# First attention of a two-layer vision tower: the last three iterations written out by hand, with other PSUM banks for the last groups' norm products

## The reference, cut to what matters

```python
tokens = jnp.einsum('bpi,hi->bph', patches, W) + b
...
logits = jnp.einsum('bhid,bhjd->bhij', q, k) * scale
logits = jnp.einsum('bhij,gh->bgij', logits, w_pre)
attn = jax.nn.softmax(logits, axis=-1)
attn = jnp.einsum('bhij,gh->bgij', attn, w_post)
out = jnp.einsum('bhij,bhjd->bhid', attn, v)
out = out.transpose(0, 2, 1, 3).reshape(b, n, dim)
return out @ w_out.T + b_out
...
m = jnp.mean(x, axis=axis, keepdims=True)
v = jnp.var(x, axis=axis, keepdims=True)
return (x - m) / jnp.sqrt(v + eps)
```

## Time and profile before

| | us |
|---|---|
| median of 3 runs | 844.15 (841.25 to 845.89) |
| the profiled execution | 846.13 |
| its span | 844.3 |
| mean granted PE clock over the span | 0.811 of full speed |

### The profile page before, as it was taken

How to read it: one execution, slowest core, us unless ns; L and a number is a source line. 1 busy time by engine, 2 the same in 40 slices (tenths; PEclk the granted TensorE clock), 3 DMA queues, 4 the chain that set the end, 5 groups by cost and what they waited for, 6 DMA issues and landing times. The chain is left out here.

```text
span 844.3 us, 21253 instructions
## 1 busy us (share of the span) xinstructions
PE 646.9 (77%) x8455; PEld 528.0 (63%) x8455; DVE 504.6 (60%) x904; ACT 349.2 (41%) x871; POOL 224.6 (27%) x254
## 2 busy tenths in 40 slices
PE   2999999999999996750799767778688888982002
PEld 2888888888888875540774556567577777761001
DVE  0375666666666665436214888768577777755862
ACT  0113444444444444230353333432566666765600
POOL 1263333333333333000000233210443333330001
PEclk9999999999999998555559987655688888875555
DMA  8443332333333100016940800000000000001200
GB/s 350 171 174 116 116 117 114 114 114 125 120 132 125 69 2 2 1 47 154 151 60 0 103 0 0 1 0 0 2 3 2 0 0 0 2 2 50 71 8 4
DMA packets 28659, 55.36 MB, mean 66 GB/s; under 512 B 12274, under 2 KB 25698, under 8 KB 26114
## 3 DMA queue, kind: packets, MB, share of 16 engines
q1 hardware_dynamic: 28515, 54.62, 21.8%
q0 software_dynamic: 96, 0.07, 0.0%
HBM read 48.14 MB, written 6.55 MB: 65 GB/s over the span
## 5 line engine op out<-in xcount | busy, mean ns | idle before, releaser
L375 PE MATMUL a_bank<-a_x,a_tok_w 128*128 128x256 f32 (+1 forms) x608 | 151.0, 391 | 15.7 <-DVE a_ht L555 15.7
L375 PEld LDWEIGHTS a_bank<-a_x,a_tok_w 128*128 128x128 f32 (+1 forms) x608 | 113.4, 192 | 37.4 <-DMA tables<-in_tables 15.7
L124 POOL TENSOR_TENSOR a_qt<-a_qp,data 128x512 f32<-128x512 f32 x64 | 71.8, 1153 | 2.1 <-POOL a_qp L617 1.6
L617 POOL TENSOR_TENSOR a_qp<-a_rope 128x260 f32<-128x260 f32 x16 | 11.7, 733 | 176.0 <-DVE a_rope L499 176.0
L1360 ACT ACTIVATE b_at<-b_bank 65x512 f32<-65x512 f32 x64 | 34.9, 602 | 42.7 <-PE b_bank L1207 42.7
L282 ACT ACTIVATE a_at<-a_bank 65x256 f32<-65x256 f32 x128 | 38.9, 390 | 26.8 <-PE a_bank L259 26.8
L493 DVE SCALAR_TENSOR_TENSOR a_ht<-a_bank,data 128x256 f32<-128x256 f32 x16 | 7.7, 484 | 64.9 <-PE a_bank L375 64.9
L259 PE MATMUL a_bank<-a_mix,a_e 64*65 64x64 f32 x1024 | 41.5, 237 | 0.0
L1444 POOL TENSOR_TENSOR b_e<-b_e,b_inv 128x585 f32<-128x585 f32 (+1 forms) x32 | 35.5, 1108 | 20.1 <-DVE b_inv L1295 19.9
L259 PEld LDWEIGHTS a_bank<-a_mix,a_e 64*65 64x65 f32 x1024 | 36.8, 149 | 4.0 <-issue 3.4
L1268 DVE TENSOR_TENSOR b_e<-b_scores,tables 128x520 f32<-128x520 f32 x32 | 20.9, 696 | 29.2 <-PE b_scores L1169 29.2
(11 more groups left out here) (251 smaller groups left out, 1552.8 us busy)
## 6 DMA issues: line engine op xcount, KB each, us to landing
a_x<-in_x SPq DMA_DIRECT2D x16, 2304.0 KB, 7.9
lag_rows<-r_kernel SPq DMA_DIRECT2D x1, 4192.5 KB, 39.0
lags<-lag_rows SPq DMA_DIRECT2D x1, 2112.5 KB
base<-places SPq DMA_DIRECT2D x1, 2080.0 KB
out<-e_plain SPq DMA_DIRECT2D x16, 130.0 KB
expert_weights<-in_w SPq DMA_DIRECT2D x2, 1024.0 KB, 5.9
a_tok_w<-in_tok_w SPq DMA_DIRECT2D x1, 1152.0 KB, 6.6
data<-in_data SPq DMA_DIRECT2D x1, 910.5 KB, 4.6
```

Source lines behind the costliest of these rows:

```text
L124: nc.gpsimd.tensor_tensor(qt[:, b * BLOCKS * P:(b + 1) * BLOCKS * P].rearrange("p (c h i) -> p c h i", i=qb, h=HEADS), wide(by_image[:, b, ...
L375: mm = nc.tensor.matmul(banks[0][:, 0:GP], w[0:rows, k * DIM:(k + 1) * DIM], x[p][0:rows, k * GP:(k + 1) * GP], start=(k == 0), stop=(k == ...
```

## The change

The pipeline generator now ends after iteration 13 on PE, DVE and ACT (POOL and SP keep theirs). What iterations 14, 15 and 16 held is written out by hand, with n = 15. No step is added or dropped; the order of steps on each engine is another, and the banks are:

- output projection, mean and variance of group 13 and of group 15 in bank 0, those of group 14 in bank 2; values of group 15 in bank 6; the last-row mix of 14 and 15 in bank 7, columns 384 on (`late_bank`);
- `centre` of group 15 writes into `rope[0]` (`late_zc`) instead of `zc`;
- helpers take the bank as an argument, `spread` is split into `square` and `root`.

The diff, cut to the part that is written out:

```diff
+            def output(g, bank):
+                pe.wait_ge(S.ot_ready, g + 1)
+                product(bank, D("wo"), ot[:, :]).then_inc(S.y_done, 1)
+
+            def mix_last_rows(g, bank):
+                pe.wait_ge(S.probs_ready, g + 1)
+                nc.tensor.matmul(bank, e[g % 2][:, SLOTS - 1, :], mix_last[:, :], start=True, stop=True).then_inc(S.mixed, 1)
...
                     values_of_image(nc, 3, at, vs[p], banks[7]).then_inc(S.av_done, 1)
 
+            n = GROUPS - 1
+            pe.wait_ge(S.qt_ready, 5 * (n + 1))
+            pe.wait_ge(S.kt_ready, n + 1)
+            pe.wait_ge(S.log_saved, n - 2)
+            scores_of_group(nc, n, seq, qt, kt, S)
+            pe.wait_ge(S.ht_ready, n + 1)
+            output(n - 2, 0)
+
+            pe.wait_ge(S.z_ready, n - 2)
+            pe.wait_ge(S.centred, n - 2)
+            pe.wait_ge(S.sd_ready, n - 2)
+            pe.wait_ge(S.v_ready, n)
+            mix_last_rows(n - 1, late_bank)
+            mix_pair(nc, pe, n - 1, 0, e[0], mix, banks[4:6], S)
+
+            pe.wait_ge(S.tok_saved, n - 2)
+            values(n, ht[1], tokens_bank)
+            pe.wait_ge(S.at_ready, 9 * (n - 1) + 5)
+            mix_pair(nc, pe, n - 1, 1, e[0], mix, banks[4:6], S)
+            values_of_image(nc, 0, at, vs[0], banks[7])
+            values_of_image(nc, 1, at, vs[0], banks[7])
+            mean(n - 2, 0)
+            pe.wait_ge(S.at_ready, 9 * (n - 1) + 9)
+            values_of_image(nc, 2, at, vs[0], banks[7])
+            values_of_image(nc, 3, at, vs[0], banks[7]).then_inc(S.av_done, 1)
+            var(n - 2, 0)
+
+            pe.wait_ge(S.shifted, 3 * n + 3)
+            output(n - 1, 2)
+            mix_last_rows(n, late_bank)
+            mix_pair(nc, pe, n, 0, e[1], mix, banks[4:6], S)
+            mean(n - 1, 2)
+            pe.wait_ge(S.at_ready, 9 * n + 5)
+            mix_pair(nc, pe, n, 1, e[1], mix, banks[4:6], S)
+            pe.wait_ge(S.v_ready, n + 1)
+            values_of_image(nc, 0, at, vs[1], banks[7])
+            values_of_image(nc, 1, at, vs[1], banks[7])
+            tail(n - 2)
+            pe.wait_ge(S.at_ready, 9 * n + 9)
+            values_of_image(nc, 2, at, vs[1], banks[7])
+            values_of_image(nc, 3, at, vs[1], banks[7]).then_inc(S.av_done, 1)
+            var(n - 1, 2)
+
+            pe.wait_ge(S.sd_ready, n - 1)
+            output(n, 0)
+            mean(n, 0)
+            pe.wait_ge(S.tok_saved, n - 1)
+            tail(n - 1)
+            var(n, 0)
+            pe.wait_ge(S.tok_saved, n)
+            tail(n)
+
...
+            n = GROUPS - 1
+            shift_scores(nc, dve, n, seq, e[1], mx, S, 3)
+            residual(n - 2, 0)
+            values(n, 1, tokens_bank)
+            normalise(nc, dve, n, e[1], total, inv, S)
+            centre(n - 2, 0)
+            residual(n - 1, 2)
+            scale(n - 2)
+            save_logits(n - 2)
+            centre(n - 1, 2)
+            residual(n, 0)
+
+            dve.wait_ge(S.q_sum, GROUPS)
+            centre(n, 0, late_zc)
+            scale(n - 1)
+            save_logits(n - 1)
+            scale(n, late_zc)
+            save_logits(n)
+
...
+            n = GROUPS - 1
+            late_zc = rope[0][:, :, :].rearrange("p b t -> p (b t)")
+            save_last(n - 1, late_bank)
+            save_pair(nc, act, n - 1, 0, banks[4:6], at, S)
+            exp_of_group(nc, act, n, e[1], S)
+            save_pair(nc, act, n - 1, 1, banks[4:6], at, S)
+            save_heads(nc, act, n - 1, banks[7], ot, S)
+            square(n - 2)
+            root(n - 2, 0)
+            save_last(n, late_bank)
+            save_pair(nc, act, n, 0, banks[4:6], at, S)
+            save_pair(nc, act, n, 1, banks[4:6], at, S)
+            square(n - 1)
+            save_heads(nc, act, n, banks[7], ot, S)
+            root(n - 1, 2)
+            save_tokens(n - 2)
+            square(n, late_zc)
+            act.wait_ge(S.inverse, n)
+            root(n, 0)
+            save_tokens(n - 1)
+            save_tokens(n)
```

More of the change, by code:

```diff
@@ L339, in embed_and_attend @@
         logit_bank = banks[1][0:TOKENS, 448:448 + GI * EXPERTS0]
+        late_bank = banks[7][0:TOKENS, 384:384 + GI * HEADS]
         x_sem = [S.x0, S.x1]
@@ L422, in _ @@
             pe.wait_ge(S.wmade, 33)
-            for g, i, p in pipeline(pe, 3, GROUPS + 1):
+            for g, i, p in pipeline(pe, 3, GROUPS - 2):
                 flat = ht[p][:, :, :].rearrange("p b t -> p (b t)")
@@ L515, in rotate_keys, with values @@
                                         rope[3][:, :, :], ALU.add).then_inc(S.kt_ready, 1)
-            def values(g, p):
+            def values(g, p, bank=values_bank):
                 dve.wait_ge(S.v_done, g + 1)
@@ L559, in _ @@
             dve.wait_ge(S.v_cleared, 2)
-            for g, i, p in pipeline(dve, 3, GROUPS + 1):
+            for g, i, p in pipeline(dve, 3, GROUPS - 2):
                 if exists(g + 1):
@@ L578, in _, with square, root, save_last @@
                     tokens(g + 3, 1 - p)
+            n = GROUPS - 1
[15 more added lines that the diff above has]
+            save_logits(n)
         @block.scalar
         def _(act):
-            def spread(g):
+            def square(g, zc=zc):
                 act.wait_ge(S.centred, g + 1)
                 nc.scalar.activation(sq[:, :], zc[:, :], ACT.Square).then_inc(S.squared, 1)
+            def root(g, bank=5):
                 act.wait_ge(S.var_done, g + 1)
-                nc.scalar.activation(sd[:, :], banks[5][:, 0:GT], ACT.Sqrt, bias=R.eps[:, :]).then_inc(S.sd_ready, 1)
+                nc.scalar.activation(sd[:, :], banks[bank][:, 0:GT], ACT.Sqrt, bias=R.eps[:, :]).then_inc(S.sd_ready, 1)
+            def save_last(g, bank):
+                act.wait_ge(S.mixed, 3 * g + 1)
+                wait_past(act, S.av_done, g)
+                nc.scalar.activation(at[0:TOKENS, :, :, PATCHES], bank.rearrange("t (b h) -> t b h", b=GI),
+                                     ACT.Copy).then_inc(S.at_ready, 1)
             def save_tokens(g):
@@ L593, in _ @@
             act.wait_ge(S.v_cleared, 3)
-            for g, i, p in pipeline(act, 1, GROUPS + 1):
+            for g, i, p in pipeline(act, 1, GROUPS - 2):
                 if exists(g + 1):
@@ L597, in _ @@
                 if exists(g - 1):
-                    spread(g - 1)
+                    square(g - 1)
+                    root(g - 1)
                 if exists(g):
-                    act.wait_ge(S.mixed, 3 * g + 1)
-                    wait_past(act, S.av_done, g)
-                    nc.scalar.activation(at[0:TOKENS, :, :, PATCHES], lastbank.rearrange("t (b h) -> t b h", b=GI),
-                                         ACT.Copy).then_inc(S.at_ready, 1)
+                    save_last(g, lastbank)
                     save_pair(nc, act, g, 0, banks[4:6], at, S)
```

25 lines of the change are left out of this document (13 added, 12 removed).

## The result

The changed kernel takes 835.29 us (median of 4 runs, 834.32 to 836.74), the kernel before 844.75 beside it (841.25 to 845.89). The ratio is 0.9893, with a 95% interval of 0.9870 to 0.9916: some 9 us faster. A second measurement of the same kernel gave 834.47 against 844.99, ratio 0.9874 (0.9857 to 0.9890). The forecast was 839.5, with a range of 834.5 to 843.3. The direction and the range hold; the gain is twice the forecast. All ratios here leave out slow executions; there was one, of the experiment exp_fill, at 1059.66 us with a granted clock of 0.55 (its median is 829.68 with it, 829.53 without it).

What follows compares the result with a forecast made beforehand. No engine was the bound; PE, DVE and ACT waited on each other, with PE's clock second. The walk fell from 375.06 to 370.36, 4.7 us gained; 846.13 less 4.7 and 1.98 to the median gave 839.5, range 834.5 to 843.3.

Steps and rivals of the forecast that it cites:

- What bounds the stage: Iterations 14 to 16, 331.26 to 375.74: no engine is the bound; PE, DVE and ACT hand work to each other.
- Costs of the steps at a given clock: Each engine's new list walked with traced durations and 0.04 us per hop; the old order's walk ends at 375.06.
- walk for PE at 1.00 to the end: If PE stays at 2.4 GHz to the stage's end, the walk ends at 362.9, gain 12.1 us.
- First leg: Group 15's scores at 331.26 to its probabilities at 342.6, PE at 2.4 GHz: 0.5 us later than before.
- The table switch: ACT's table load before exp of 15: taken as 1.28 us, at most 1.62; rival of dearer switch, chance 0.04.
- The drain: The skill page adds about 1.38 us per table switch; not used in the forecast, with it 840.9.
- Second and third leg: Second: to the logits of 13, copied by 353.8, PE the path. Third: norms of 14 and 15, to 370.36.
- I take the clock as falling here, at 344.5: Behind the projection of 14 PE's clock falls, later pieces cost 1.2 GHz prices; gain 4.7 us.
- a clock of 1.00 through 345 to 352: Named sign, in the new trace, that the forecast is wrong.
- the rival that I had given 0.25 and 836.0: PE's packed work keeps its clock up between 344.5 and 351.4: 3.4 us more, gain 8.1; chance 0.25.
- The rival on the slower side: PE slow from the start, its clock rising a few us later: gain about 2.5 us, 841.7; chance 0.22.
- The reference point: Profiled execution 846.13 less 4.7 is 841.4; the runs' median lies 1.98 below the profiled one, giving 839.5.

Runs made afterwards that it cites:

- exp_fill: Changed kernel with exp of group 15 back ahead of group 14's saves, and filler products ahead of the last two tails (4 and 3): 829.68 us, ratio 0.9811.
- new_fill: Changed kernel with extra 260-column products into an unread bank ahead of the variance of 13 and the tails of 14 and 15: 833.10 us, ratio 0.9861.
- old_fill: Kernel before, old order and banks, with 17 useless 260-column products in PE's waits of iterations 14 to 16: 837.44 us, ratio 0.9912.
- serial_norms: Changed kernel with the norms of 14 and 15 put back one behind the other on PE, DVE and ACT: 837.81 us, ratio 0.9906.
- tail_back: Changed kernel with PE's tail of group 13 moved back ahead of the second mix of group 15: 836.01 us, ratio 0.9898.
- old_banks: Kernel before, old order, with only the change's banks and no root wait ahead of the last two last-row products: 844.22 us, ratio 0.9998.
- exp_first: Changed kernel with ACT's exp of group 15 put back ahead of the last-row save and first four saves of group 14: 831.39 us, ratio 0.9847.
- exp_fill_centre: exp_fill with, besides, the centring of 14 ahead of the logit copy of 13 on DVE: 829.26 us, ratio 0.9810.
- exp_centre: exp_fill_centre without the fillers: 830.54 us, ratio 0.9829.

## Why the prediction was right in sign and range, and half the size

*What bounds the stage: right.* No engine was the bound, and rearranging lists without removing one instruction took a quarter of the stage.

*Costs of the steps at a given clock: right within about a microsecond.* The prediction's walk for PE at 1.00 to the end was 362.9 less 331.26, 31.6 us; new_fill took 31.92, 0.9 of it for fillers that were in the way. For the old order the expectation of old_fill gave 36 us, and it took 37.07. The difference, 4 to 5 us by the expectation, measured 4.3 in the medians and 5.2 in the profiles.

*First leg: right to half a microsecond.* Counted from the first score, the first mix of 14 started at 3.0 us (forecast 3.2), exp at 6.7 (6.8), the centring of 13 at 10.9 (11.3). The idle ahead of the variance of 13 was 2.00 us (2.0), ahead of the last tail 2.95 (2.85). That the exp had gone on the path was named and priced at 0.5 us against the old order. What I did not ask is what it costs against the best order: moving it back gave 3 to 4 us.

*The table switch: right to take 1.28.* The prediction could only bound it by 0.34 us from above. In the new order nothing hides it, and the exps follow 0.01 us behind the load. The drain that the Trainium skill (ScalarE: Activation LUTs, What ACT_TABLE_LOAD costs) adds, about 1.38 us, is not there.

*Second and third leg: the clock, wrong.* The step that failed is that everything behind "I take the clock as falling here, at 344.5" was priced at 1.2 GHz to the end. That the clock falls there was right. It fell at 343.1, at that very place in PE's list, but came back at 346.5, after 3.4 us, during the mean of 14. The tail of 13 began at 18.3 us from the first score instead of 20.3, the reciprocal of 14 at 23.4 instead of 28.1, that of 15 at 28.6 instead of 34.1, and the end came at 33.5 instead of 39.1 (370.36 less 331.26). Of the missing 5.6 us 0.4 were there at the centring of 13. The rest is about what the prices of the two levels give for the pieces on the path: the second mix of 15 (0.9), two images (0.4), the tails of 13 and 14 (1.0 and 0.9), the variance of 14, the projection and the mean of 15 (0.6 each). One of the signs that I had named for being wrong, a clock of 1.00 through 345 to 352, is met in the most part of that stretch.

That was the rival that I had given 0.25 and 836.0. Its time is near the measured one partly by luck: it had the first mix of 15 at 2.4 GHz, which ran at 1.2, and everything from 351.4 on at 1.2 GHz, where the clock stayed up to 356.7.

*Why the clock came back is open.* In all four profiles of kernels with the 2.00 us wait ahead of the variance of 13 (the change twice, serial_norms, tail_back) it fell 10.4 to 13.4 us after the first score and was back 3.4 or 6.8 us later. Work without gaps is not enough to explain it. In the new order PE had no idle time from 342.2 to 346.7; but in the old order it had none either in two longer stretches, and the clock stayed at 1.2 GHz through both (the second lies in the stretch from 351 to 366 that I had set against this rival):

```profile
344.40:349.30 4.90, 4.90 (x76) 0.50 0.00 0
357.14:364.40 7.26, 7.26 (x110) 0.50 0.01 2
```

The pieces differ (mixes, tails and attention output there; variance, projection, mix and mean here), and old_banks shows the old order with its clock back from 348.9. No run separates the kind of the work from where it happens to fall. What is shown is that the clock, held up by fillers, is worth 7.5 us to the old order and 1.4 to 2.2 to the new one. The sentence of the Trainium skill that I had set beside this rival (TensorE: Matmul & The Clock Gate, What's actually happening: activity releases the throttle) agrees with old_fill in so far as activity without any use kept the clock up; the two stretches above show that it does not by itself give the place.

*The rival on the slower side did not arise.* PE was at 1.00 when the stage began in every profile but that of tail_back, where it came up within 0.2 us. But the rise had come only 0.2 to 1.0 us ahead of the first score in the others, so this was close.

*The reference point.* The forecast went by the median of 844.15; beside the experiments the kernel before measured 844.68 to 844.99, 0.5 to 0.8 us more. By that the forecast would have been about 840.2: a small miss in the same direction as the large one.

## What to carry to other kernels

Where engines hand work to each other and none is the bound, walk the new lists with the traced durations: it gave the order's worth within a microsecond. But PE's clock moved with the order: here the order gave about 4.3 us and the clock about 5 more. So the walk should be made at both levels, and a rise in the middle should be given its weight, not only a fall. Before moving an instruction, ask what stands behind it in its queue: a table load and three exps placed behind five saves cost 3 to 4 us here, where the choice of banks by itself made no difference.

## What the runs showed of the hardware that I had not expected

- Useless work made a kernel faster: 17 products placed in PE's waits took 7.5 us off the old order, with PE's clock at 2.4 GHz for all 37 us of the stage instead of about 10 of 44.
- The clock fell in the change at the same place in both profiles, 12.8 and 13.4 us after the first score of 15, behind the 2.00 us wait for the square of 13. It fell near there in serial_norms (13.0) and tail_back (10.4, in the wait) too. With that wait cut to 0.81 us (exp_first, exp_fill, exp_fill_centre, exp_centre) or filled down to 0.50 (new_fill) it did not fall there.
- PE was busy without a gap for 7.26 us of the old order (357.14 to 364.40), and the clock stayed at 1.2 GHz all through it; it came back at 365.0.
- The same old order went through this stage in 44.5 us in one profile and, with banks that made no difference in the medians, in 41.0 in another, with the clock back for 17 us behind the first fall instead of 3.4.
